# A vision transformer layer with experts: q and k spread from SBUF to SBUF instead of through memory, and list entries of 64 bytes

## The reference

```
h = emb(x / 255)                         # [64, 197, 192]
q, k, v = split(h @ w_attn + b_attn)     # 12 heads x 16
att = softmax(causal(q k^T / 4))
h = LN(h + (att v) @ w_proj + b_proj)
for k in (0, 1):                         # best two experts of each token
    buf[expert, position] = token        # at most int(1.2 * N / 8) per expert
    out += weight * (silu(x W1[:, H:]) * (x W1[:, :H])) W2
h = LN(h + out)
```

## Time and profile before

| | |
|---|---|
| median of 3 runs | 2357.99 us (2357.78 to 2363.21) |
| the profiled execution | 2355.76 us |
| its span | 2354.0 us |
| mean granted clock of PE | 0.965 |
| PE busy | 2140.5 us (91%) |
| DVE, ACT, POOL busy | 1590.6, 1083.2, 1576.6 us |
| DMA moved | 219.72 MB in 232530 packets |

### The profile page before, as it was taken

The page is one execution under the profiler, slowest core; times in us unless marked ns, Lnnn a source line. Parts: engine busy times, 40 slices in busy tenths (PEclk is TensorE's granted clock), DMA queues, the critical chain, the costliest instruction groups (busy, mean ns, idle before and its releaser), DMA issues. The chain is left out here.

```text
span 2354.0 us, 48984 instructions
## 1 busy us (share of the span) xinstructions
PE 2140.5 (91%) x14772; PEld 2070.2 (88%) x14772; DVE 1590.6 (68%) x4287; ACT 1083.2 (46%) x2840; POOL 1576.6 (67%) x2326
## 2 busy tenths in 40 slices
PE   4999999999999999999999559999999999999990
PEld 4899898999989999999988459999999999999980
DVE  4577777877777777777777436666666666666556
ACT  2344444444444444444444225454545454544545
POOL 3356676767666767676765557777777777767666
PEclk9999999999999999999999679999999999999995
DMA  5658888776676565655643133201010101000338
GB/s 155 153 119 123 137 127 142 130 133 137 140 124 139 135 135 136 134 137 133 139 111 84 34 112 62 44 6 26 2 29 3 28 3 26 2 2 15 54 48 332
DMA packets 232530, 219.72 MB, mean 93 GB/s; under 512 B 91027, under 2 KB 212754, under 8 KB 231376
## 3 DMA queue, kind: packets, MB, share of 16 engines
q1 hardware_dynamic: 134800, 146.55, 26.7%
q10 hardware_dynamic: 43328, 56.78, 12.9%
q0 software_dynamic: 54272, 14.76, 5.1%
HBM read 152.91 MB, written 95.25 MB: 105 GB/s over the span
## 5 line engine op out<-in xcount | busy, mean ns | idle before, releaser
L1162 POOL DMA_INDIRECT x_tokens<-yout,e_entry x240 | 382.0, 1592 | 182.1 <-DVE yout L1348 133.5
L651 PE MATMUL Y<-p,vp 128*102 128x198 f32 x1536 | 361.0, 344 | 17.6 <-ACT ysb L482 13.0
L443 POOL DMA_INDIRECT expert_lists<-entry,slot x256 | 288.1, 1126 | 54.1 <-issue 54.1
L1363 DVE TENSOR_TENSOR a<-UP,gate 128x384 f32<-128x384 f32 x320 | 178.6, 558 | 211.7 <-ACT gate L1300 169.8
L487 ACT ACTIVATE p<-ST 128x396 f32<-128x396 f32 x384 | 191.7, 499 | 264.5 <-PE ST L623 247.9
L1255 PE MATMUL Y<-w,a_hi 128*128 128x384 f32 x960 | 304.4, 354 | 2.0 <-DVE a_lo L1353 2.0
L1142 POOL DMA_INDIRECT rows<-x_wide,e_entry x240 | 250.3, 1043 | 77.4 <-issue 72.4
L1300 ACT ACTIVATE gate<-GT 128x384 f32<-128x384 f32 x320 | 157.6, 492 | 290.1 <-PE UP L1242 267.8
L141 POOL TENSOR_TENSOR word_p<-word_p 1x1 f32<-1x1 f32 x416 | 85.8, 206 | 304.6 <-ACT p L489 295.3
L409 POOL TENSOR_TENSOR x_lo<-x,x_hi 128x396 fp32r<-128x396 f32 x192 | 208.2, 1086 | 91.1 <-ACT x_hi L465 89.0
L651 PEld LDWEIGHTS Y<-p,vp 128*102 128x102 f32 x1536 | 221.6, 170 | 32.2 <-issue 11.4
(11 more groups left out here) (181 smaller groups left out, 6400.1 us busy)
## 6 DMA issues: line engine op xcount, KB each, us to landing
x<-in_xt ACTq DMA_DIRECT2D x180, 198.0 KB
q<-qk_features SPq DMA_DIRECT2D x384, 74.2 KB
k<-qk_features SPq DMA_DIRECT2D x192, 148.5 KB
qk_features<-qk_hi SPq DMA_DIRECT2D x96, 198.0 KB
qk_features<-qk_lo SPq DMA_DIRECT2D x96, 198.0 KB
e_raw<-in_wexp SPq DMA_DIRECT2D x8, 1408.0 KB, 6.7
rb<-rd ACTq DMA_DIRECT2D x128, 74.2 KB
t_x<-x_tokens SPq DMA_DIRECT2D x15, 576.0 KB, 7.5
```

The lines of the kernel that those rows point to most:

```text
L443: pool.indirect_dma_start(d["lists"][:, :], bass.IndirectOffsetOnAxis(ap=slot[o][0:REAL[t], t, c:c + 1], axis=0), entry[o][0:REAL[t], t, c ...
L651: return pe.matmul(Y[0:VW1, 0:TI], v0, p32[b][:, hh, 0:TI], start=start, stop=stop)
L1162: pool.indirect_dma_start(d["x1"][:, :], row_of(cc, t), yout[q][:], None, bounds_check=N - 1, oob_is_err=False, compute_op=ALU.add)\
L1363: dve.tensor_tensor(a32[m % 2][:], UP[m % 2][:, 0:TILE3], gate[m % 2][:], ALU.mult)\
```

## The change

The array in memory for q and k goes, with its stores. The columns of the q and k weights are put in another order on the host, so that a product's first 96 features are one third of q or k in "wide" form (QK0: q of the first head of every head pair, QK1: q of the second, QK2: k of the first) and its last 32 features are one third of k of the second heads. SP spreads them straight from `qk_hi` and `qk_lo`: `spread_wide` from 96 partitions into 16 partitions of six rows each, `spread_third` from 32 partitions into 16 partitions of two rows each. For image 0 they are issued as soon as the product is drained (after steps 3, 4 and 6 of SP's order), three of each for one product; for image 1, all eighteen, after the wait for the turned scores in step 9. A pair has 36 spreads and no store. ACT waits before QK0 for all spreads of the pair before, both images.

The rows of x1 are stored in step 0 of the next body with six DMAs, each for both images. A list entry has 64 bytes (16 floats, of which two are used), the blank tile has 24 entries a partition and is repeated ten times by the clearing DMA, which ACT issues behind the first rounding of x.

```diff
-ROW = 2
+ROW, BLANK = 16, 24
...
-            def store_qk(g, par, t):
...
+            def spread_wide(par, im, t):
+
+                cols = slice(im * TI, (im + 1) * TI)
+                for c, from_lo in enumerate(((0, 0, 1), (0, 0, 1), (0, 1, 0))[t]):
+                    row = 2 * HD * c + (HD if t == 1 else 0)
+                    dst = q[par][row:row + HD, im, t] if t < 2 else k[par][row:row + HD, im]
+                    src = (qk_lo if from_lo else qk_hi)[t][0:CH, cols]
+                    sp.dma_start(dst.bitcast(F32), src.bitcast(F32)).then_inc(s_qkr[im][par], 16)
+
+            def spread_third(par, im, t):
+
+                cols = slice(im * TI, (im + 1) * TI)
+                for c, from_lo in enumerate((0, 1, 0)):
+                    row = 2 * HD * c + HD
+                    src = (qk_lo if from_lo else qk_hi)[t][CH:P, cols]
+                    sp.dma_start(k[par][row:row + HD, im, 2 * t:2 * t + 2].bitcast(F32), src.bitcast(F32))\
+                        .then_inc(s_qkr[im][par], 16)
...
+                    if s == 0 and 5 in stages:
+                        p = i - 4
+                        sp.wait_ge(s_x1, p + 1)
+                        for hf in range(2):
+                            src = pay[par][0:REAL[hf], hf::2, :]
+                            x1_rows, xin_rows = rows_of("x1", p, hf), rows_of("xin", p, hf)
+                            for dst, part in ((x1_rows, src), (xin_rows[:, :, 0:C], src),
+                                              (xin_rows[:, :, C:XW], src[:, :, P:C])):
+                                sp.dma_start(dst, part).then_inc(s_st1[par], 16)
+                    if s in (3, 4, 6) and 1 in stages:
+                        t = (3, 4, 6).index(s)
+                        if t == 0:
                             sp.wait_ge(s_qset, 5)
+                            wait(sp, s_st, (i - 2) * STEPS + 6)
+                        g.wait_drained(sp, f"QK{t}")
+                        spread_wide(par, 0, t)
+                        spread_third(par, 0, t)
...
                     if s == 9 and 1 in stages:
                         wait(sp, s_st, (i - 1) * STEPS)
-                        spread_q(par, 1)
-                    if s == 10 and 1 in stages:
-                        spread_k(par, 1)
+                        for t in range(3):
+                            spread_wide(par, 1, t)
+                            spread_third(par, 1, t)
...
-            act.wait_ge(s_blank, 1)
-            act.dma_start(d["lists"].rearrange("(p a) c -> p (a c)", p=P),
-                          blank[:].rearrange("p a c -> p (a c)")).then_inc(s_clear, 16)
...
             act.wait_ge(s_x, 16 * KT)
             for t in range(KT):
                 x_round(0, t)
+            act.wait_ge(s_blank, 1)
+            act.dma_start(d["lists"].rearrange("(p n a) c -> p n (a c)", p=P, a=BLANK),
+                          blank[:].rearrange("p a c -> p (a c)").unsqueeze(1)
+                          .broadcast_to([P, NSLOT // P // BLANK, BLANK * ROW])).then_inc(s_clear, 16)
...
                             if t == 0:
-                                wait(act, s_qkw[1 - par], (turn + par) * (QW * 16))
+                                for im in range(2):
+                                    wait(act, s_qkr[im][1 - par], (turn + par) * (QR * 16))
...
-    d["qk"] = nc.dram_tensor("qk_features", [2, 2, 2, 2 * C, TI], F32).ap()
...
-    by_row = np.arange(C).reshape(NH // 2, 2 * HD).T.ravel()
-    order = np.concatenate([by_row, C + by_row, 2 * C + np.arange(C)])
+    by_row = np.arange(C).reshape(NH // 2, 2, HD).transpose(1, 2, 0)
+    thirds = C + by_row[1].reshape(HD, 3, 2).transpose(1, 0, 2)
+    wide = (by_row[0], by_row[1], C + by_row[0])
```

More of the change, by code:

```diff
@@ L226, in attention_block @@
         half = sb("half", [P, 4], F32)
-        blank = sb("blank", [P, NSLOT // P, ROW], F32)
+        blank = sb("blank", [P, BLANK, ROW], F32)
         word_v, word_p = sb("word_v", [1, NWORDS], F32), sb("word_p", [1, NWORDS], F32)
@@ L281, in attention_block @@
         s_hhi, s_hlo, s_qkhi = sem("h_hi_part"), sem("h_split"), sem("qk_hi_part")
-        s_qkw = [sem("qk_stored0"), sem("qk_stored1")]
         s_qkr = [[sem(f"qk_spread{im}_{n}") for n in range(2)] for im in range(2)]
@@ L302, in attention_block @@
         SETS = 12
-        QW, QR = 6, 9
+        QR = 18
         def body_at(i):
@@ new lines, in spread_third, with rows_of @@
+            def spread_third(par, im, t):
[5 more added lines that the diff above has]
+                        .then_inc(s_qkr[im][par], 16)
+            def rows_of(name, p, hf):
+                view = d[name].rearrange("(n m t) c -> n t m c", m=2, t=T)
+                return view[p, hf * P:hf * P + REAL[hf]]
@@ L363, in body @@
                 for s in range(STEPS):
[L364 to L367, removed]
-                            sp.wait_ge(s_qset, 5)
[L369 to L385, removed]
+                    if s == 0 and 5 in stages:
[7 more added lines that the diff above has]
+                                sp.dma_start(dst, part).then_inc(s_st1[par], 16)
@@ L389, in body @@
-                    if s == 10 and 1 in stages:
-                        spread_k(par, 1)
+                        for t in range(3):
+                            spread_wide(par, 1, t)
+                            spread_third(par, 1, t)
             run_bodies(sp, body)
             for par in range(2):
-                sp.wait_ge(s_st1[par], NPAIR // 2 * 12 * 16)
+                sp.wait_ge(s_st1[par], NPAIR // 2 * 6 * 16)
         @block.gpsimd
@@ L549, in body @@
                                 done = turn - 2 + par
-                                act.wait_ge(s_st1[o], done * 12 * 16)
+                                act.wait_ge(s_st1[o], done * 6 * 16)
                                 act.wait_ge(s_sc[o], done * 8 * 16)
@@ L946, in body @@
                             done = turn - 2 + par
-                            dve.wait_ge(s_st1[o], done * 12 * 16)
+                            dve.wait_ge(s_st1[o], done * 6 * 16)
                             dve.wait_ge(s_sc[o], done * 8 * 16)
@@ L1431, in halves @@
         return w.reshape(2, CH, -1).transpose(1, 0, 2)
-    by_row = np.arange(C).reshape(NH // 2, 2 * HD).T.ravel()
-    order = np.concatenate([by_row, C + by_row, 2 * C + np.arange(C)])
+    by_row = np.arange(C).reshape(NH // 2, 2, HD).transpose(1, 2, 0)
+    thirds = C + by_row[1].reshape(HD, 3, 2).transpose(1, 0, 2)
+    wide = (by_row[0], by_row[1], C + by_row[0])
+    order = np.concatenate([np.concatenate([wide[t].ravel(), thirds[t].ravel()]) for t in range(3)]
+                           + [2 * C + np.arange(C)])
     wa, ba = np.asarray(L0_attn_w_attn)[:, order], np.asarray(L0_attn_b_attn)[order]
```

## The result

The changed kernel takes 2375.9 us (median of 7 runs, 2370.4 to 2381.1); the kernel before, run beside it, 2358.4 (2357.8 to 2366.6). The ratio is 1.0067, with 95% between 1.005 and 1.0084. The forecast was 2371. The medians are of executions in the fast state; two executions, of 5335 and 9901 us, one each of two experiments, are left out of them. The profiled execution of the changed kernel has a span of 2378.3 us, 24.3 more than before.

A forecast was written before the change was run, and what follows sets the result against it. It took the matmul engine PE as the bound, with only the pipeline's filling or a long new wait able to move the time: 13.6 + 1.5 - 2.0 + 0.2 = +13.3 us on 2357.99, so 2371; four-fifths range 2349 to 2400.

The forecast's parts named there:

- four signs: Expected in the trace: spreads 0.78 to 0.80 us, first scores near 57, ACT's qk_hi near 72 and 105, rounds 39.1.
- The issue of one spread: On SP's queue: one SBUF-to-SBUF spread takes 0.82 us from start to start, bounds 0.44 and 0.92.
- The first rounds: Pipeline start: ACT's QK0 waits for all 36 spreads of the pair before; 13.6 us later, plus 1.5 for half clock.
- The filling: The pipeline's start-up rounds, where PE first idles 6.04 us; forecast to lose 13.6 us plus 1.5 at half clock.
- In between: Rival for SP's issue price: 0.55 to 0.7 us a spread, about 2357 us in all, no change; chance 0.17.
- The full pipeline: Later rounds: image 1's spreads land 1.7 us in time, x1's moved stores delay nobody, rounds stay at 39.1 us.
- 2 us of relief: Full pipeline: emptier DMA engines give PE back up to 3.3 us of waits, taken as 2.
- The wait in every round: Rival: at 0.92 us an issue or more, ACT waits for spreads each round; 2378 to about 2425 us; chance 0.13.
- The lists: Later, larger clearing store and 64-byte entries: 0 us each; larger list loads: +0.2 us once.
- those 3.3 us: PE's waits for DMAs from 100 to 1280 us: 3.0 for the row of maxima, 0.3 for k; limit of gain.
- The sum: Whole kernel: 13.6 + 1.5 - 2.0 + 0.2 = +13.3 us on the median of 2357.99, giving 2371.

The follow-up runs named there:

- The probe: Changed kernel with x1's stores cut, plus 28 transfers of seven partition shapes on SP, then on ACT; issues took 0.56 to 0.64 us, with 12 partitions 0.75 to 0.81.

## Why the prediction was right, and where it was not

The direction was right and the time of 2371 lay 5 us under the measured 2376, but it came about for other reasons than the forecast gave; that the time was met is luck. Of the four signs that it named none came as said: the spreads take 0.60 us and not 0.78 to 0.80, PE's first scores are at 53.98 and not near 57, ACT's qk_hi of pairs 1 and 2 at 65.4 and 94.0 and not 72 and 105, and not all rounds last 39.1. Only that ACT waits there for a DMA of k was so. Step by step:

- **The issue of one spread**, forecast at 0.82 us a start, was 0.64. This is a term that was mis-sized. I took the price of rb and of the row of maxima, because they too go from SBUF to SBUF with different partition counts. The probe shows that what makes the row of maxima dear is its shape, 12 partitions on a side (0.77), not the change of partition count (96 to 16: 0.64) nor the queue. For rb, 6 partitions to 96, it has no such shape; 6 to 6 takes 0.68 where rb takes 0.78, so its price is explained only in part. The Trainium skill's rule, which I weighed and set aside because of the 69-row store, pointed the right way for 12 partitions. It was not the whole answer, since even with 16 engines SBUF to SBUF costs more than the spread from memory at 0.42.
- **The first rounds.** The working stood, the price did not. With 0.64 in its formula, 39.92 + 36 x 0.64 + 2.6 = 65.6 for ACT's QK0 of pair 1; measured 65.37. The filling cost 3.6 us, not 15.1.
- **"In between" was the rival that the issue price fulfilled**, and it would have given 2357. It was off by 19 us because it shared the step that comes next.
- **The full pipeline** was forecast unchanged, with 2 us of relief. This is the step that failed, by some 22 us (the rounds took 19.9 more where 2 less was forecast): "x1's stores, moved past the image 1 spreads to the next round, are wanted by nobody within that round". True of who wants them, but the price lay with what is issued behind them. I counted the issues of the moved step on its own queue, and not the engines that its transfers hold, nor what ACT issues 0.5 us later on the other queue. The cut to 64 and 5 rows shows it: some 34 us.
- **The wait in every round** was the right rival to keep. Its limit, 0.92 us an issue, was worked out for a queue with nothing ahead of the image 1 spreads; with the 12 stores ahead it decides at 0.64 already. That it is ACT's wait for all spreads of an image at once is shown by the kernel with waits by product and the stores in step 8.
- **The lists** were forecast at 0 to 0.5 us. They save 11 us in the kernel before and 16 with the cut stores; in the changed kernel itself the runs don't tell. I costed POOL's issue and the last landing, and not what small writes do to other packets. The 0.84 of DMA share at 134 GB/s in the early rounds stood in the trace, and I did not ask whether those engines were busy with bytes. Nor was the pipeline as full as the one stretch of 39.1 us suggested: the rounds of the kernel before last 39.6 us on average, up to 42.7, and beside the waits named in the forecast PE waited 11.7 us in 41 waits for ysb, ACT's copy of the value product:

```profile
PE Y L651 <- ACT ysb L482: 11.7, 41, 0.6
```

So "worth at most those 3.3 us" was too low a limit for what emptier DMA engines can give.

- **The sum** came right because two misses cancelled in part: on one side the filling, 11.5 us too dear, and the lists' gain left out (11 to 16), on the other the held-up row of maxima left out (some 34). As a chain of medians: 2348 before; 2357 with direct spreads, the new place and the cut, but the old lists; 2341 with the new lists too; 2374 with the stores not cut.

What stays open: why the long rounds alternate with short ones and why the clock falls in only some of them, why entries of 8 bytes hold up other packets, and what sets the issue price between 0.42 (from memory), 0.56 (96 to 96) and 0.64 (96 to 16).

## What to carry to other kernels

Count for a moved DMA not only its issues but the engines that it lands on: a transfer whose row count has no large divisor up to 16 (69 = 3 x 23) sits on few engines, and a small, urgent transfer issued behind it, on another queue too, can wait for the slowest of them; cutting it to 64 + 5 cost three issues a pair and gave some 34 us. A wait for a whole group of transfers should be as fine as the buffers that they free: one semaphore a product instead of one for three was worth 149 us where the queue was late and nothing where it was not. And when DMA share is high at a modest rate, look for the small writes before removing bytes: 39 MB less moved gave nothing, wider list entries gave 11 to 16 us.

## What the runs showed of the hardware

- The issue of a transfer from SBUF to SBUF takes 0.56 to 0.64 us where both partition counts divide by 16, 0.75 to 0.81 with 12 partitions on a side, 0.68 for 6 to 6; alike on SP's and ACT's queue.
- Behind a hole of 1.7 us in PE's work the granted clock was 0.65 for 5 us (long round from 570.70), and that round is 1.5 us longer than one with the same hole and the clock at 1.00 (42.5 and 41.0 us). Eight of twelve such holes had it.
- Behind a store of 69 rows, which ran some three packets at a time, a row of twelve shares issued 0.5 us later on another queue landed nine shares within 2.9 us and the last three only 6.1 to 7.1 us after its issue.
- With scattered entries of 8 bytes the average packet of two other kinds takes 1.4 to 1.8 times as long as with entries of 64 bytes (511 and 356 ns, 197 and 107 ns, from 205.6 to 440 us), by a minority of packets that take over 1 us; the median packet is no slower, and from 1000 us on the difference is gone.
